# All eight experts in sixteen sorted tiles, with the rows of the first four tiles gathered by a product with ones and zeros

## The reference, cut to what matters

```python
# xf: 576 tokens x 192; 8 experts; the best 2 of each token are kept
logits = xf @ Wrouter
topk_w, topk_idx = jax.lax.top_k(logits, 2)
topk_w = jax.nn.softmax(topk_w, axis=-1)
we = jnp.zeros((N, 8)).at[jnp.arange(N)[:, None], topk_idx].add(topk_w)
def body(acc, expert):
    W1e, W2e, we_e = expert                    # 192 x 768, 768 x 192
    h = jax.nn.gelu(xf @ W1e, approximate=False)
    return (acc + we_e[:, None] * (h @ W2e), None)
```

## Time and profile before

| | us |
|---|---|
| three runs, median | 407.72 |
| lowest, highest | 403.25, 407.98 |
| the profiled execution | 402.83 |
| its span | 401.0 |
| its expert block, from the first instruction to the last | 296.4 to 401.0 |

### The profile page before, as it was taken

One profiled execution on the slowest core, in us unless ns is written; L12 is line 12 of the kernel. 1 busy time (PEld: TensorE's weight loads), 2 busy tenths in 40 slices (PEclk: granted clock), 3 DMA queues, 4 the chain that ended last, 5 costly groups with the idle time before them and its releaser, 6 DMA issues. The chain is left out here.

```text
span 401.0 us, 8441 instructions
## 1 busy us (share of the span) xinstructions
PE 361.2 (90%) x2724; PEld 287.7 (72%) x2724; DVE 275.4 (69%) x654; ACT 237.1 (59%) x641; POOL 128.1 (32%) x161
## 2 busy tenths in 40 slices
PE   8999799999998789999888999787959889999994
PEld 5336466666668678887776777665859679999983
DVE  1668799999972673446886438788647649765656
ACT  3566878988850406676455366666437177866640
POOL 2101413333300431425564216555366002121100
PEclk9999899999999999999999999999879989999998
DMA  8374434345404600699000065200235546300031
GB/s 164 54 228 95 101 102 106 95 126 125 116 14 118 251 1 0 213 287 260 25 2 2 2 254 189 82 3 2 81 83 186 174 163 203 120 12 21 3 101 45
DMA packets 23424, 42.19 MB, mean 105 GB/s; under 512 B 4772, under 2 KB 17092, under 8 KB 23256
## 3 DMA queue, kind: packets, MB, share of 16 engines
q1 hardware_dynamic: 21848, 39.46, 34.7%
q0 software_dynamic: 1024, 1.97, 1.4%
q10 hardware_dynamic: 512, 0.24, 0.2%
HBM read 38.29 MB, written 9.27 MB: 119 GB/s over the span
## 5 line engine op out<-in xcount | busy, mean ns | idle before, releaser
L557 PE MATMUL ps<-weights,hT 120*96 120x288 f32 x320 | 81.6, 411 | 0.9 <-DVE weights L395 0.9
L557 PEld LDWEIGHTS ps<-weights,hT 120*96 120x96 f32 x320 | 51.7, 166 | 24.8 <-DVE weights L395 1.5
L395 DVE SCALAR_TENSOR_TENSOR weights<-dist_y,hat_x 120x576 f32<-120x576 f32 x80 | 60.4, 795 | 1.7 <-PE ps L557 1.2
L1133 ACT ACTIVATE a_probs<-ps,a_minus_peak 108x108 f32<-108x108 f32 (+1 forms) x144 | 47.2, 340 | 11.0 <-DVE a_minus_peak L1196 11.0
L1293 POOL TENSOR_TENSOR a_probs_n<-a_probs,a_inv_sums 108x324 f32<-108x324 f32 (+1 forms) x48 | 39.1, 815 | 42.0 <-DVE a_inv_sums L1203 41.0
L314 POOL TENSOR_TENSOR h_step<-h_act 96x600 f32<-96x600 f32 x14 | 26.6, 1899 | 69.7 <-DVE weights L395 69.7
L464 ACT ACTIVATE dist_y<-pos,row_shift 120x576 f32<-120x576 f32 x64 | 46.8, 769 | 1.4 <-DVE weights L395 1.0
L1775 PE MATMUL ps<-slot_w,hT_hi 128*128 x90 | 27.8, 371 | 4.2 <-DVE hT_lo L1986 3.9
L1904 POOL DMA_INDIRECT yk_dram<-x,dest x12 | 12.6, 1047 | 59.5 <-DVE x L1997 59.5
L1133 ACT ACTIVATION_READ_ACCUMULATOR a_probs<-ps,a_minus_peak 108x1 f32 (+1 forms) x144 | 29.5, 205 | 0.0
L1196 DVE TENSOR_REDUCE a_minus_peak<-ps 108x3 f32<-108x324 f32 (+1 forms) x48 | 21.4, 447 | 8.8 <-PE ps L1025 8.7
(11 more groups left out here) (222 smaller groups left out, 873.5 us busy)
## 6 DMA issues: line engine op xcount, KB each, us to landing
pos<-pos_dram SPq DMA_DIRECT2D x16, 540.0 KB, 4.5
raw<-in_w SPq DMA_DIRECT2D x8, 768.0 KB, 4.5
xg_dram<-in_pad SPq DMA_DIRECT2D x1, 5304.0 KB, 22.7
raw<-in_w SPq DMA_DIRECT2D x7, 576.0 KB
patches<-in_patches SPq DMA_DIRECT2D x6, 216.0 KB, 5.7
hid<-xg_dram SPq DMA_DIRECT2D x9, 136.0 KB, 2.4
dcn_w<-in_dcn_w SPq DMA_DIRECT2D x1, 1152.0 KB, 11.2
yk_dram<-in_pad SPq DMA_DIRECT2D x1, 864.0 KB, 27.8
```

The source lines that it names most:

```text
L395: nc.vector.scalar_tensor_tensor(weights[:, t, :], dist_y[:, t, :], 1.0, hat_x[:, s, :], ALU.min, ALU.mult).then_inc(weights_ready, 1)
L557: ins = nc.tensor.matmul(ps[0:C1, 2 * (b % 2) + a, 0:HALF], hT[:, b % 2, t, :], weights[:, t, a * HALF:(a + 1) * HALF], start=(t == 0), st ...
L1133: nc.scalar.activation(probs[0:n, u % 3, j, 0:n], ps[0:n, u % 4, j * n:(j + 1) * n], ACT.Exp, bias=minus_peak[0:n, u % 4, j:j + 1], accum_ ...
```

## The change

Expert 0 is sorted as well: there are 16 tiles, and the dense computation of expert 0 is gone; short products with zeros (`fill`) stand in some of its places. The rows of tiles 0 to 3 are no longer transposed from DRAM: rows of all tokens are split in two halves (`rows_high` on ScalarE, `rows_low` on VectorE), VectorE compares each token's place with 128 row numbers (`find`, 128x640 ones and zeros), and TensorE multiplies (`tile_finds_x`, 20 products of 128 columns for a tile). Gates and destinations of these tiles still come from DRAM, in four small loads (`load_meta`) and a step of VectorE (`meta_first`) ahead of `tile_y(0)`. Tiles 4 to 15 come as before. The W1 of expert 3 is split in the attention layer too; W1 of 4 to 7 and all eight W2 are split in the expert block. W2 has three raw buffers. In the attention block one scatter is left, and one addition goes from GpSimd to VectorE. In the second batch, `places` comes behind two `find`s and `gates` last.

```diff
-TILES_E = (2 * NTOK + (EXPERTS - 1) * 127) // 128
+TILES_E = (2 * NTOK + EXPERTS * 127) // 128
+RAW_2 = 3
+FIRST_E = 4
-EARLY_SPLITS = {4: ("high", 0), 5: ("low", 0), 6: ("rest", 0), 8: ("high", 1), 9: ("low", 1), 10: ("rest", 1), 14: ("high", 2), 18: ("low", 2), 22: ("rest", 2)}
-TURN_ACT = {0: [(1, 5), (2, 4)], 1: [(1, 6)], 2: [(2, 5)], 3: [(1, 7)], 4: [(2, 6)], 5: [(2, 7)]}
-TURN_DVE = {1: [(1, 5), (2, 4)], 2: [(1, 6)], 3: [(2, 5)], 4: [(1, 7)], 5: [(2, 6)], 6: [(2, 7)]}
+EARLY_SPLITS = {3: ("high", 0), 4: ("low", 0), 5: ("rest", 0), 6: ("high", 1), 7: ("low", 1), 8: ("rest", 1), 9: ("high", 2), 10: ("low", 2), 11: ("rest", 2), 14: ("high", 3), 18: ("low", 3), 22: ("rest", 3)}
+TURN_ACT = {1: [(2, 3)], 2: [(1, 5), (2, 4)], 3: [(1, 6), (2, 5)], 4: [(2, 6)], 5: [(1, 7)], 6: [(2, 7)]}
+TURN_DVE = {0: [(2, 1)], 1: [(2, 2)], 2: [(1, 4), (2, 3)], 3: [(1, 5)], 4: [(2, 4), (1, 6)], 5: [(2, 5)], 6: [(1, 7), (2, 6)], 7: [(2, 7)]}
...
# attention block, layer 1: TensorE
-                    up_ahead(nc, pe, P, following, 0)
+                    fill(nc, P, 4)
                     output(XT - 1)
                     transpose_x(XT - 2)
                     route_counts(nc, pe, P, following, 0)
-                    up_ahead(nc, pe, P, following, 1)
-                    up_ahead(nc, pe, P, following, 2)
+                    fill(nc, P, 8)
                     transpose_x(XT - 1)
...
# VectorE
                     tail(XT - 2, 1)
+                    tail(XT - 1, 0)
+                    n = XTILES[XT - 1][1]
+                    nc.vector.tensor_tensor(P["rest"][0:n, XT - 1, :], P["h"][0:n, XT - 1, :], P["x"][0:n, XT - 1, :], ALU.add)
                     gates(nc, dve, P, following, 0)
-                    tail(XT - 1, 0)
+                    tail(XT - 1, 1)
                     places(nc, dve, P, following, 0)
-                    tail(XT - 1, 1)
...
# GpSimd
                     scatter_rows(nc, P, following, 0, 0)
-                    scatter_rows(nc, P, following, 0, 1)
-                    base(XT - 1)
...
+def fill(nc, P, times):
+    for _ in range(times):
+        nc.tensor.matmul(P["ps"][:, 4, 0:256], P["zeros"][:, 0:128], P["zeros"][:, :], start=True, stop=True)
...
# expert block: SyncE
+                next_w2(3)
+                sp.wait_ge(map_ready, 2)
+                sp.wait_ge(W["scattered"], 16 * 2 * XT)
+                load_meta(0)
+                load_rows(FIRST_E)
+                for i in range(1, FIRST_E):
+                    load_meta(i)
+                for i in range(FIRST_E + 1, FIRST_E + SET):
+                    load_rows(i)
+                next_w2(4)
+                for i in range(FIRST_E + SET, FIRST_E + 2 * SET):
+                    load_rows(i)
+                next_w2(5)
+                next_w1(6)
...
# TensorE
+                def tile_finds_x(i):
+                    pe.wait_ge(W["rows_lo_done"], 3)
+                    pe.wait_ge(found, i + 1)
+                    if i >= 1:
+                        pe.wait_ge(tile_xT_copied, DC * i)
+                    for c in range(DC):
+                        at = slice(c * 128, (c + 1) * 128)
+                        for t, (t0, n) in enumerate(XTILES):
+                            for a, half in enumerate((rows_hi, rows_lo)):
+                                ins = nc.tensor.matmul(ps[:, 7, at], half[0:n, t, at], found_at[i][0:n, t, :], start=(t == 0 and a == 0), stop=(t == XT - 1 and a == 1))
+                    ins.then_inc(tile_xT_ready, 1)
...
-                for f in range(3, FT):
-                    up_ahead(nc, pe, P, W, f)
+                fill(nc, P, 6)
                 route_counts(nc, pe, P, W, 1)
                 totals()
-                for f in range(FT):
-                    up_late(f)
-                for t in range(XT):
-                    down(t)
-                tile_transposes_x(0)
-                tile_transposes_x(1)
+                fill(nc, P, 12)
+                tile_finds_x(0)
+                tile_finds_x(1)
                 for i in range(TILES_E):
                     tile_ups(i)
-                    if i + 2 < TILES_E:
+                    if i + 2 < FIRST_E:
+                        tile_finds_x(i + 2)
+                    elif i + 2 < TILES_E:
                         tile_transposes_x(i + 2)
...
# ScalarE ahead of the tiles: all gelu_part gone
+                w2_high(0)
                 w2_high(1)
                 w1_high(4)
                 copy_xT(0)
                 copy_xT(1)
+                w2_high(2)
...
# VectorE ahead of the tiles
-                w2_low(1)
+                rows_low(nc, dve, W, 0)
                 best_two(nc, dve, P, W, 1)
                 choices(nc, dve, P, W, 1)
-                w2_low(2)
+                rows_low(nc, dve, W, 1)
+                tile_map()
+                find(0)
+                find(1)
+                places(nc, dve, P, W, 1)
+                slots()
                 gates(nc, dve, P, W, 1)
-                places(nc, dve, P, W, 1)
-                tile_map()
-                w1_low(3)
-                ...
                 tile_split_x(0)
+                find(2)
+                w2_low(0)
                 tile_split_x(1)
                 for i in range(TILES_E):
+                    if i == 0:
+                        find(FIRST_E - 1)
                     if i >= 1:
                         tile_low(i - 1)
...
+                    if i == 1:
+                        meta_first()
                     if i >= 1:
                         tile_y(i - 1)
```

More of the change, by code:

```diff
@@ new lines, in stage_experts @@
+        apart = sb("apart", [128, XT, EXPERTS])
+        apart_of = gelu_out[:, 1, 0:FIRST_E * XT * EXPERTS].rearrange("p (i t e) -> p i t e", i=FIRST_E, t=XT)
+        place_of = sb("place_of", [128, FIRST_E, XT])
+        place_in = sb("place_in", [128, FIRST_E, XT])
+        rows_hi, rows_lo = rows_halves(W)
+        found_at = [W["slot_lo1"][:, slot, 0:XT * 128].rearrange("p (t j) -> p t j", t=XT) for slot in (4, 5, 6, 5)]
+        first_meta = sb("first_meta", [128, FIRST_E, 2 * EXPERTS])
@@ L1666, in _ @@
-                next_w1(6)
-                for i in range(SET, 3 * SET):
+                sp.wait_ge(map_ready, 2)
[6 more added lines that the diff above has]
+                    load_rows(i)
+                next_w2(4)
+                for i in range(FIRST_E + SET, FIRST_E + 2 * SET):
@@ L1668, in _ @@
                     load_rows(i)
                 next_w2(5)
+                next_w1(6)
+                for i in range(FIRST_E + 2 * SET, FIRST_E + 3 * SET):
+                    load_rows(i)
+                next_w2(6)
                 next_w1(7)
-                next_w2(6)
-                for i in range(3 * SET, 4 * SET):
+                next_w2(7)
+                sp.wait_ge(w2_done, 6)
+                sp.dma_start(all_tokens, D["tokens"]).then_inc(tokens_loaded, 16)
+                for i in range(FIRST_E + 3 * SET, TILES_E):
@@ L1673, in _ @@
                     load_rows(i)
-                next_w2(7)
-                for i in range(4 * SET, TILES_E):
-                    load_rows(i)
-                sp.wait_ge(w2_done, EXPERTS - 1)
+                sp.wait_ge(w2_done, EXPERTS)
                 sp.wait_ge(W["w1_lo_done"], EXPERTS)
@@ L1887, in _ @@
             def _(pool):
-                ahead = [(k, t) for k in range(2) for t in range(*BATCHES[0])][2:]
-                for k, t in ahead[0:2]:
+                ahead = [(k, t) for k in range(2) for t in range(*BATCHES[0])][1:]
+                for k, t in ahead[0:3]:
                     scatter_rows(nc, P, W, k, t)
                 second_power(nc, pool, W, 1)
-                for k, t in ahead[2:]:
+                for k, t in ahead[3:]:
                     scatter_rows(nc, P, W, k, t)
@@ L1935, in tile_map @@
[L1935 removed]
+                    route.done(nc.vector.tensor_tensor(of_tile[:, :, :], begun[:, :, 0:EXPERTS], begun[:, :, 1:], ALU.subtract))
+                    route.done(nc.vector.scalar_tensor_tensor(apart[:, :, :], W["chosen"][:, :, :], -float(APART), ps[:, 3, COUNTS_AT:COUNTS_AT + XT * EXPERTS].rearrange("p (t e) -> p t e", t=XT), ALU.mult, ALU.add))
                     route.wait()
[L1937 removed]
@@ L1938, in tile_map @@
-                    route.done(nc.vector.tensor_scalar(around[:, :], tile_expert[:, :], float(SLOTS_2 + 1), -float(SLOTS_2), ALU.is_ge, ALU.mult))
-                    nc.vector.tensor_scalar(slot1_at[:, :], tile_expert[:, :], -1.0, None, ALU.add).then_inc(map_ready, 1)
+                    route.done(nc.vector.tensor_tensor(shifted[:, :, :], of_tile[:, :, :], shift[:, :].unsqueeze(1).to_broadcast((128, TILES_E, EXPERTS)), ALU.mult))
+                    route.done(nc.vector.tensor_tensor(apart_of, of_tile[:, 0:FIRST_E, :].unsqueeze(2).to_broadcast((128, FIRST_E, XT, EXPERTS)), apart[:, :, :].unsqueeze(1).to_broadcast((128, FIRST_E, XT, EXPERTS)), ALU.mult))
@@ L1940, in tile_map @@
                     route.wait()
```

(16 more changed lines are left out.)

293 lines of the change are left out of this document (124 added, 169 removed).

## The result

| | before | after |
|---|---|---|
| median of 20 runs, us | 403.98 | 409.73 |
| lowest, highest | 398.10, 408.15 | 404.11, 415.91 |
| the profiled execution | 402.83 | 411.84 |
| its span | 401.0 | 410.1 |
| its mean granted clock | 0.971 | 0.948 |

The ratio of after to before is 1.0153, 95% interval 1.0113 to 1.0192. That is within 2%, and the interval leaves out 1: the kernel became about 6 us slower. I had forecast 1.6 us more, and 409 in all; that this is within 1 us of the 409.73 measured is luck, since it was added to a median of 407.7 for the kernel before, which came out at 403.98 here.

The account below looks back on a forecast made before the run. TensorE bounded the steady tiles before, VectorE would after. 9.2 us earlier and 1.5 of clock saved, against 4.4 (tile), 4.0 (finds), waits 6.9 for 2.5, rest rounding: 1.6 more, 407.7 + 1.6 = 409.3, rounded to 409; range 400 to 416.

Parts of the forecast that it names:

- no wait in turn 1: Sign of being wrong: in turn 1 of the sorted tiles, TensorE's forecast 2.6 us stand ahead of `tile_downs(1)` is missing.
- The new wait: Expert block, turn 1: last meta lands at T+28.4, so VectorE stands 3.2 us and TensorE 2.6 ahead of `tile_downs(1)`.
- T: Start of the expert block, forecast at 295.6 us; the prediction counts its later times from it.
- Rival (c): Expert block: the gather buys nothing, tile 0's results wait for the same DRAM trip; 407.3 us, chance 0.15.
- rival (a): Expert block: TensorE stays the bound, meta in time, waits 2.5 us, warm clock in the first find; 401.7 us, chance 0.2.
- The first find to the first `tile_ups`: Start of the expert block: first find's products 3.6 us, to T+11.9, second to T+15.1; `tile_ups` at 310.7, 9.2 us earlier.
- VectorE as the bound: Expert block, turns 2 to 6: VectorE's splits make TensorE wait 1.4, 1.3 and 1.6 us ahead of `tile_downs` 2, 3, 4.
- The border: Between attention and expert block: one scatter and one addition leave GpSimd, so the expert block begins 1.3 us earlier (0 to 1.9).
- the splits: Attention block, turns 3, 7 and 11: three more W1 splits on VectorE cost 0.5 us in all (0 to 2.8).
- Rival (b): Expert block: the gates, scatter, meta chain decides and the clock falls ahead of `tile_downs(1)`; 8.2 us over before, 416, chance 0.2.
- the walk: Expert block: going through the engines' streams in order to the last `tile_ups`, T+89.2, with 1.4 us added T+90.6, 386.2 us.
- the tail: From the last `tile_ups` to the span's end: 16.4 us, nothing in it changes.

Follow-up runs that it names:

- e9: Changed kernel with ten products instead of twenty in each find, the low halves of the rows left out; ratio to the kernel before 1.0143.
- e11: Changed kernel with half the products of each find and a copy in place of W2's low-half subtraction; ratio to the kernel before 1.0085.
- e10: Changed kernel with a copy in place of VectorE's subtraction for W2's low half, which then holds other numbers; ratio to the kernel before 1.0136.
- e6: Changed kernel with second-batch places and gates ahead of the tile map and first finds, and 36 filling products for 12; ratio to the kernel before 1.0172.
- e5: Changed kernel with 36 instead of 12 filling products ahead of the first find; ratio to the kernel before 1.0149.
- e4: Changed kernel with second-batch places and gates ahead of the tile map and first two finds; ratio to the kernel before 1.0335.
- e1: Kernel before with the changed kernel's early W1 splits, expert 3's W1 no longer split in the expert block; ratio to the kernel before 0.9970.
- e3: Changed kernel with all 30 filling products of zeros left out; ratio to the kernel before 1.0201.
- e2: Changed kernel with the same twelve W1 split steps spread over attention turns 4 to 22; ratio to the kernel before 1.0315.

## Why the prediction was right, and where it wasn't

The forecast was 1.6 us more, with 6 measured by the medians: within 2% and on the right side, as forecast, and short by 4 us. The mechanism was right only in part. Of the prediction's own signs of being wrong all three came: no wait in turn 1, the first `tile_ups` at 319.06 for 313 at most, and the border at 299.15 for 296 at most. That the sum came so near owes something to luck, as errors of both signs stand in it. By its steps:

**The new wait** (gates, scatters, last meta; VectorE stands 3.2 us and TensorE 2.6 ahead of `tile_downs(1)`): it did not come. The gates ended at T+12.0 for a forecast T+11.1, and the last meta was issued by T+27.4 for T+26.3, so the chain itself went as worked out. But VectorE came to its step only at 332.10, T+33, because the finds had pushed everything behind. The wait was hidden by a greater delay. In e9, with the finds halved, it shows again: VectorE stands 1.06 us ahead of the first step on meta and TensorE 0.64 us ahead of `tile_downs(1)`; in e11 it is 1.52 and 1.11. So the wait is real, and for the changed kernel it was the length of the finds, at the clock that they had, that decided. Rival (c), which was this wait alone, falls with it. Of rival (a) the first half came, the meta in time and TensorE's work setting the pace; the warm clock in the first find, which it took as given, did not.

**The first find to the first `tile_ups`** was the step that failed: T+8.0 to T+15.1 were forecast, T+9.4 to T+19.9 came. Of these 4.8 us 1.4 are a later start (VectorE waited 1.39 us for the totals' products; in e9 it was 0.21), 0.6 the first find, and 2.8 the second, which I had at the full clock after the first had run. The clock was 0.53 over the stretch. Besides, a product is 0.135 us at the full clock, not the 0.11 that I read from the transposes in the earlier trace rows; at the low one 0.25, not 0.21. That makes the third and fourth find 5.6 us for 4.4. By the Trainium skill (TensorE: Matmul & The Clock Gate, "Wait — 56ns, not 53.3ns?"), which gives about 56 ns for 128 columns of bf16, an estimate for a find would be 1.1 us; this trace's fp32r finds take 2.70.

**VectorE as the bound** (TensorE waits 1.4, 1.3 and 1.6 ahead of `tile_downs` 2, 3 and 4, none after): found at 1.01, 0.68 and 1.15, at those three places and no other until the last two tiles. This mechanism was right, and smaller by 1.5 us (2.8 for 4.3). From the first to the last `tile_ups` I had 75.5 us, and it was 73.9; that these are near each other is luck. The 2.6 us ahead of `tile_downs(1)` and these 1.5 did not come, while the two finds took 1.2 us more and the clock was still at 0.50 for the first 3.7 us, which I had not counted. In e10 a lighter W2 step took 0.6 us off the waits.

**The border** (1.3 us earlier) and **the splits** (0.5 us later, together 0.8 earlier): in e6, e9 and e10, with the clock at 1.00 through the first 50 us of it and a low stretch of some 3.3 us behind that, as in before, the attention block was 0.4 to 0.7 us shorter than before's, for a forecast of 0.8. (In e5, with no such stretch, it was 1.9 shorter; in e4, with two of them, 0.7 longer.) The splits' own cost was 0.1 by turn 12 (e1). `normalise` did take 1.35 us in the turns 3 and 7 and 1.50 in turn 11, for 0.73 before, but the turns had room for it. These lengths agree with the Trainium skill (SBUF — State Buffer, "SBUF: two separate sides"), by which such a VectorE step and a GpSimd one exclude each other; the price that the prediction worked out from it, 1.9 us in all, did not come. What I had not counted is the fall of the clock at 254.7, 2.7 us in the profiled execution. Of the eleven profiled executions with this table of splits it came at this place, 21 us into the block, in three (after, e3 and e11), so it is no steady cost.

**Rival (b)** had the clock fall, but ahead of `tile_downs(1)`; it fell at the finds. e4 shows what it is like where it lasts.

**The sum**: 1.6 us forecast; first `tile_ups` +4.8, the walk -1.6, the tail +0.7: the block 3.9 us longer than forecast, which makes 5.5, near the 5.75 between the medians. Between the profiled spans there are besides the attention block, 2.2 us longer for 0.8 shorter, and its later start of 0.5: 9.0 of the 9.1 us. How much of either the median execution has, no profile shows.

**What stays open**: why the clock falls at 254.7 in some executions, and why the finds' stretch stays at the low clock as long as it does. No run separates the kind of product from the gaps ahead of it. No run holds the clock at 1.00 through both finds ahead of `tile_ups`, so what the finds would cost then is not measured. Nor was a find of fewer products with rows as exact as before tried.

## What to carry to other kernels

A gather by products with ones and zeros is bought with TensorE's time, at the clock that TensorE has just then: price it at both levels, and take the price from products of the same type and length. Work that hides a latency and is also needed (here the dense expert) is a cover at no cost; taking it away saves only what it cost beyond the sorted tiles that replace it, and here left the engine standing in the same place, at a low clock. When one delay is taken out, look at once for the wait behind it, and for what freed the buffer and not only for the queue: here a load of W1 that could not start before the split of an earlier W1 had ended. And compare two profiles' lengths only beside their clocks: low stretches of 3.3 us came and went between kernels that differ elsewhere.

## What the runs showed of the hardware

- The granted clock stayed at 0.50 for 17.69 us in which TensorE is shown busy throughout (e4), and for 17.62 us in e10. In e5 a find of 2.85 us and a stand of 0.99 us, in which the clock fell, were followed by a find of 5.07 us.
- With the same attention block, the profiled executions of after, e3 and e11 had the clock fall 21 us into it and those of e5, e6, e9 and e10 did not. After's own twenty executions had mean clocks from 0.935 (415.91 us) to 0.968 (404.11 us). With other turns for VectorE's splits (e2) it was 0.61 over 52 us.
- A product of 128 columns with its own weights, both fp32r, takes 0.135 us from start to start at the clock of 1.00 and 0.25 at 0.50 (after, 20 products in 2.70 and 5.00 us).
- The step that waits for the totals' five products began 1.2 us behind their shown end in after and e5 (302.93 to 304.15 in after), and at once in e3, e9 and e10 (0.21 us of wait). What the 1.2 us are is open; matmul ends are modelled.
